# A recurrent attention layer and a mixture of experts on one core: expert weights split once and kept in f16, token tiles of 128 rows in unrolled code, and two normalisations moved to ScalarE

## The reference

```python
# block 1: linear attention with a decaying 64x64 state per head (4 heads, batch 2)
inter = einsum('bij,bcj->bci', W, rk_c) * g_p            # read of the state
S     = einsum('bcd,bkd->bck', rk_c, wk_c)               # keys are the reads, one token late
intra = einsum('bck,bkd->bcd', S * M, v_c)               # within the chunk, decayed and causal
W_new = g_C * W + einsum('bci,bcj->bij', v_c * g_w, wk_c)
x = x + out + (alpha * reads) @ W_read.T                 # out = layernorm(x)
# block 2: top 2 of 8 experts for each of 4096 tokens, width 1024
probs = softmax(layernorm(x) @ gate_w.T); p, idx = top_k(probs, 2)
h = gelu(x1n @ w1[e].T + b1[e]); y = h @ w2[e].T + b2[e] # for both chosen e
x = x + sum_k p_k * y_k
```

## Time and profile before

| | us |
|---|---|
| median of the 3 timed runs | 681.88 |
| span of the profiled execution, first to last instruction | 644.7 |
| difference: what lies around the span | 37.2 |
| PE busy | 585.2 (91%) |
| DVE busy | 560.0 (87%) |
| ACT busy | 414.1 (64%) |
| POOL busy | 291.4 (45%) |

### The profile page before, as it was taken

The page is one execution under the profiler, slowest core; times in us unless marked ns, Lnnn a source line. Parts: engine busy times, 40 slices in busy tenths (PEclk is TensorE's granted clock), DMA queues, the critical chain, the costliest instruction groups (busy, mean ns, idle before and its releaser), DMA issues.

```text
span 644.7 us, 17218 instructions
## 1 busy us (share of the span) xinstructions
PE 585.2 (91%) x5368; PEld 502.0 (78%) x5368; DVE 560.0 (87%) x1323; ACT 414.1 (64%) x819; POOL 291.4 (45%) x301
## 2 busy tenths in 40 slices
PE   3899889888894499999999999999999999999992
PEld 2677677676673288888888888888888888888882
DVE  4699898998886799999999998999999999999971
ACT  6454554543541487878777777777787877777751
POOL 4145777677667414443343434243433334342433
PEclk9899997999896599999999999999999999999997
DMA  6567464466122415253434434252524343443422
GB/s 231 185 201 280 134 229 165 161 224 205 60 94 96 97 29 84 48 76 51 73 57 67 71 53 77 47 82 47 77 49 74 51 73 57 67 72 52 80 29 33
DMA packets 87098, 63.46 MB, mean 98 GB/s; under 512 B 56224, under 2 KB 79392, under 8 KB 87072
## 3 DMA queue, kind: packets, MB, share of 16 engines
q1 hardware_dynamic: 72768, 44.23, 25.4%
q0 software_dynamic: 14304, 18.92, 17.0%
HBM read 27.36 MB, written 25.53 MB: 82 GB/s over the span
## 4 chain that ended last, share of the span: by engine, by line
PE 61%; POOL 12%; issue 11%; DVE 8%; DMA 5%; ACT 2%; POOLq 0%; DVEq 0%; ACTq 0%; SPq 0%
PE psum L1213 28%; PE psum L1194 28%; POOL sent_rows L469 6%; DMA out<-arena 3%; POOL tiny L448 2%; DMA sent_rows<-arena,tiny 2%; DVE arena L903 2%; POOL arena L477 2%; POOL out L494 1%; PE psum L1139 1%; POOL tiny L445 1%; PE psum L1113 1%; PE psum L1142 1%; DVE arena L819 1%; PE psum L1103 1%
## 5 line engine op out<-in xcount | busy, mean ns | idle before, releaser
L1194 PE MATMUL psum<-arena 128*128 128x256 f16 x1872 | 229.7, 273 | 0.7 <-ACT arena L631 0.7
L1213 PE MATMUL psum<-arena 128*128 128x256 f16 x1872 | 229.5, 273 | 0.4 <-DVE arena L996 0.4
L1009 DVE SCALAR_TENSOR_TENSOR arena<-weights,arena 128x1024 f16<-128x1024 f16 x156 | 190.2, 1221 | 25.0 <-issue 14.1
L494 POOL DMA_INDIRECT out<-arena x78 | 133.3, 1709 | 155.9 <-ACT arena L670 135.4
L1194 PEld LDWEIGHTS psum<-arena 128*128 128x128 f16 x1872 | 183.0, 98 | 23.1 <-DVE arena L1009 0.9
L1213 PEld LDWEIGHTS psum<-arena 128*128 128x128 f16 x1872 | 183.1, 98 | 21.9 <-DVE arena L996 0.7
L651 ACT ACTIVATE arena<-weights 128x1024 f16 x156 | 164.2, 1055 | 35.8 <-PE psum L1213 20.8
L631 ACT ACTIVATE arena<-psum,arena 128x256 f32<-128x256 f32 x312 | 130.7, 470 | 68.3 <-PE psum L1194 63.6
L996 DVE TENSOR_TENSOR arena<-arena 128x512 f16<-128x512 f32 x156 | 108.1, 693 | 5.3
L469 POOL DMA_INDIRECT sent_rows<-arena,tiny x64 | 63.7, 995 | 41.4 <-DVE tiny L778 21.6
L503 POOL COPY arena<-arena 128x2 int32<-128x2 int32 x39 | 24.4, 625 | 107.6 <-DMA out<-arena 98.8
(11 more groups left out here) (129 smaller groups left out, 566.6 us busy)
## 6 DMA issues: line engine op xcount, KB each, us to landing
weights<-in_experts SPq DMA_DIRECT2D x16, 1024.0 KB
arena<-in_b SPq DMA_DIRECT2D x39, 128.0 KB, 2.9
out<-arena SPq DMA_DIRECT2D x17, 256.0 KB, 2.4
arena<-in_x SPq DMA_DIRECT2D x16, 256.0 KB, 2.8
sent_rows<-pad SPq DMA_DIRECT2D x8, 265.0 KB, 7.5
out<-arena POOLq DMA_INDIRECT x78, 4.1
sent_rows<-arena,tiny POOLq DMA_INDIRECT x64
arena<-sent_rows SPq DMA_TRANSPOSE x39, 3.9
```

The costliest lines, as they stand in the source:

```text
L494: pool.indirect_dma_start(out=out, out_offset=bass.IndirectOffsetOnAxis(ap=tok_cur[:, 1 - par, c:c + 1], axis=0), in_=yout[:, 1 - par, c], ...
L1009: v.scalar_tensor_tensor(out=wcur[:, 1 - par, w + PIECE:w + 2 * PIECE], in0=weights[:, bass.ds(e * EW + part * PIECE, PIECE)], scalar=WSCA ...
L1194: last = pe.matmul(ps_h[:, s, mm], w1_of(par, k, lo, m), tileT[:, par, part], start=(n == 0), stop=(n == 3 * KD - 1))
L1213: last = pe.matmul(ps_y[:, par, c], lhs, w2_of(par, m, lo), start=(m == 0 and n == 0), stop=(m == MF - 1 and n == 2))
```

## The change

- `TILE` is 128: `NT` becomes 71, and a tile is one group of 128 rows.
- `weights` holds f16. Stage one splits each piece once, two pieces a step: ACT `split_high(2*(n-1))` and `split_high(2*(n-1)+1)`, DVE `split_low` of the same, in place, one piece's place behind the f32 source. `wcur` and its splits in stage two are gone.
- Stage two is not a loop: 71 tiles are written out. PE reads the tile's expert from the table (`value_load`) and addresses each 128 columns of w1 and each 256 columns of w2 by a register.
- `first` has four blocks of 128 hidden units a bank and moves 128 tokens; `second` has 128 tokens stationary. Bias b2 of all experts is loaded once; the gate is folded into `finish` on DVE. Tiles are loaded four ahead; POOL adds one group of rows a tile, each after the one before it has landed.
- Both normalisations go to ACT as Identity with scale and bias; POOL computes the bias (`shift`) with two small operations more for each.
- The state is 64 columns wide (`ps_state` 128x2x2x64), `faded` is gone, and DVE updates the state with `decayC` itself; reads within the chunk are issued as one group of 64-column matmuls ahead of the group that reads the state.

```diff
-TILE = 256
+TILE = 128
-EW = 4 * PIECE
+EW = 4 * 2 * PIECE
...
+            def split_high(j, m, mp):
+                loaded(a, w_in[mp], m, mp)
+                reached(a, "wlo_done", j - 1)
...
+                a.activation(to, frm, ACT.Copy, scale=WSCALE).then_inc(S["whi_done"], 1)
...
+                if active(n, 0):
+                    reached(a, "shift1_done", n)
+                    reached(a, "xT_ps", n - 2)
+                    reached(a, "res_done", n - 2)
+                    for b in range(B):
+                        last = a.activation(xn[:, par, b], xt[:, par, b], ACT.Identity, scale=rs1[:, b:b + 1],
+                                            bias=shift1[:, b:b + 1])
...
+                if active(n, 3):
+                    m = n - 3
+                    reached(a, "shift2_done", m)
...
+                        last = a.activation(xm[:, 1 - par, b], res_of(m)[:, b], ACT.Identity, scale=rs2[:, b:b + 1],
+                                            bias=shift2[:, b:b + 1])
...
-                        pool.tensor_scalar(ve, moments[:, :, 1], EPS, None, ALU.add).then_inc(S[mid], 1)
+                        pool.tensor_scalar(ve, moments[:, :, 1], EPS, None, ALU.add)
+                        pool.tensor_scalar(shift, moments[:, :, 0], -1.0, None, ALU.mult).then_inc(S[mid], 1)
...
+                        reached(pool, end, m)
+                        pool.tensor_tensor(shift, shift, rs, ALU.mult).then_inc(S[last], 1)
...
+            def split_low(j):
+                reached(v, "whi_done", j)
...
+                v.scalar_tensor_tensor(out=lo, in0=frm, scalar=WSCALE, in1=hi, op0=ALU.mult,
+                                       op1=ALU.subtract).then_inc(S["wlo_done"], 1)
...
-                    for side in range(2):
-                        d = slice(side * HD, (side + 1) * HD)
-                        last = v.tensor_tensor(state[d, :, :, d].rearrange("p b k i -> p (b k) i"),
...
+                    for k in range(KD):
+                        last = v.scalar_tensor_tensor(out=state[:, :, k], in0=state[:, :, k], scalar=decayC[:, k:k + 1],
+                                                      in1=ps_state[:, :, k], op0=ALU.mult, op1=ALU.add)
...
+            def w1_of(e, k, lo, m):
+                return halves[:, bass.ds(e * EW + ((2 * k + lo) * PIECE + m * P), P)]
+            def w2_of(e, m, lo):
+                return halves[:, bass.ds(e * EW + ((2 * (2 + m // 4) + lo) * PIECE + m % 4 * D), D)]
...
+            def first(i, e, q):
+                if q == 0:
+                    pe.wait_ge(tileT_ld[i % 4], (i // 4 + 1) * 16)
+                came(pe, "act_done", i - 1, 2, q)
+                for mm in range(4):
+                    n = 0
+                    for k in range(KD):
+                        for lo, part in ((0, k), (0, KD + k), (1, k)):
+                            last = pe.matmul(ps_h[:, q, mm], w1_of(e, k, lo, 4 * q + mm), tileT[:, i % 4, part],
+                                             start=(n == 0), stop=(n == 3 * KD - 1))
...
+            def second(i, e, q):
+                s = 2 * (i % 2) + q
+                came(pe, "split_done", i, 2, q)
+                if q == 0:
+                    came(pe, "yout_done", i - 2)
+                for mm in range(4):
+                    for n, (half, lo) in enumerate(((h_hi, 0), (h_hi, 1), (h_lo, 0))):
+                        last = pe.matmul(ps_y[:, i % 2], half[:, s, mm], w2_of(e, 4 * q + mm, lo),
...
+            for i in range(NT + 1):
+                if has(i):
+                    e_of[i] = pe.value_load(tile_exp_i[0:1, i:i + 1], min_val=0, max_val=E - 1)
+                    first(i, e_of[i], 0)
+                if has(i - 1):
+                    second(i - 1, e_of[i - 1], 0)
+                if has(i):
+                    first(i, e_of[i], 1)
+                if has(i - 1):
+                    second(i - 1, e_of[i - 1], 1)
```

466 lines of the change are left out of this document (172 added, 294 removed).

## The result

The changed kernel takes 780.69 us (778.19 to 783.33, 4 runs) and before 682.09 (680.44 to 683.91, 4 runs): a ratio of 1.143, with a 95% interval of 1.138 to 1.148. The forecast was 703, in a range of 664 to 738. The side was right, and so was the reason (PE's sequencer). The size was not.

A forecast was written before the change was run, and what follows sets the result against it. The prediction took PE to bound stage two and DVE stage one, with PE's sequencer setting the new stage two's pace. Span 644.7 +25 -3 +1.5 -2 = 666, with 37.2 around it 703 us, range 664 to 738.

The forecast's parts named there:

- stage two: Stage-two term: 71 tiles of 6.13 us, set by PE's sequencer, 435 us against 410.4, so +25 us.
- stage one and between: Stage one -3 us (bounds -8 and +12), steps going from 11.6 to about 10.95 us; larger table and first tile's wait +1.5.
- end: End of the kernel: one add in place of two and no gate on ACT, -2 us.
- sum of the span: Whole profiled span: 644.7 us with +25 -3 +1.5 -2 gives 666 us.
- Stage two, PE's sequencer: Stage two: 48 register operations, table read and waits take 6.13 us a tile against the array's 5.30; chance 0.56.
- 109 whatever follows: PE's sequencer, stage two: a register operation costs 109 ns start to start; array instructions behind it add about 2 ns each.
- The bound from above, 120 ns: Stage two: highest price of one register operation, 57 + 63 = 120 ns, which would give 462 us.
- PE's queue evens `first` against `second`: Stage two: the queue offsets `first` (3.6 us operations, 2.7 array) against `second` (1.8, 2.6) but can't hide the sum.
- Stage two, PE's array: Stage two: 128-column matmuls at 56 ns, so the array needs 5.30 us a tile, 377 us in all, 33 less.
- the array decides: Stage-two rival: register operations hidden or under 95 ns, 377 us there, 645 in all; chance 0.24, wholly or nearly (645 to 678).
- stage one gets longer by port contention: Stage-one rival: DVE splits and POOL operations share one port, no step gain, +15 to +20 us, 722 in all; chance 0.12.
- With the 37.2 us around it: Base of the sum: 37.2 us outside the profiled span, added to 666 to give 703.4 us.

The follow-up runs named there:

- e9: The kernel before, unchanged, run a third time, on the slower kind of chip: 677.2 us, 0.999 of before.
- e10: The changed kernel again, unchanged, in a set where before takes 680.04 us: 780.5 us, 1.150 of before.
- e2: The changed kernel with addresses of coming groups worked out ahead in pairs, two to a fused operation of six parts: 646.0 us, one execution.
- e1: The changed kernel with expert 0's weights for every tile, so no table read or register operation on PE: 648.7 us, one execution.
- e13: The changed kernel with each address worked out one matmul group before the group that uses it: 751.2 us, 1.104 of before.
- e3: The kernel before with only the two normalisations moved to ScalarE, with POOL's shift operations: 691.1 us, one execution.
- e4: The changed kernel with its 32 weight splits moved out of stage one to between the stages: 840.8 us, one execution.

## Why the prediction was wrong

Against e9 and e10, which share a chip, and step by step:

| term | forecast | measured | from |
|---|---|---|---|
| stage two | +25 | +101.5 | 410.4 to 511.9 |
| stage one and between | -3 +1.5 | +3.6 | 252.0 to 255.6 |
| end | -2 | -2.1 | 11.9 to 9.8 behind the last matmul |
| sum of the span | +21.5 | +103 | 674.3 to 777.2 |

The two traces are single executions, and those of before spread over 8 us in that set. By the medians (780.50 and 680.04) the difference is 100.5, so that stage one and between come to about +1: the term lies between +1 and +4.

**Stage two, PE's sequencer: the right step, mis-sized.** The failed step is the price of a register operation, "109 whatever follows", plus 0.003 for the array instructions, in a tile of 6.13 us. Measured are 0.124 and 7.21 us (mean of 40 tiles of the trace). Of the 1.08 us between:

- 48 x 0.012 = 0.58 are this price. The reading of the earlier trace rows was right for its row: that operation, with a semaphore instruction behind it, starts 109 ns before it (250.765 and 250.874). Wrong was "whatever follows", at 2 ns for each array instruction. In the changed kernel it is 124 behind one matmul and behind two, in e2 132 where nothing stands between and 152 with three or six matmuls: array instructions behind an operation cost 15 to 20 ns once. Spread over the 24 of the earlier trace rows, such a sum looks like 2 ns each. The bound from above, 120 ns, was too low too. Each ns was known to be worth 3.4 us, so 12 ns are 41 us.
- 0.13 to 0.15 are the table read: 0.53 and a wait of 0.11 were forecast; from TENSOR_LOAD at 500.986 to the next operation at 501.777 it is 0.79.
- 0.38 weren't in the sum at all: the pauses on every eighth operation. They add 10 to 160 ns to the 124, stand in `first` (71% of their time, with 67% of the operations) and in `second` alike, and recur every 8 operations, 12 loads and 12 matmuls, so every 32 instructions of PE; the longest, about 155, returns after some 62 operations. They are tied to the count of instructions, not to a full queue or a wait. Whether it is the fetching of the unrolled code, no run tells; in e1 and e2 the array sets the pace and hides them.

"PE's queue evens `first` against `second`" held: in `second`, where the array (2.6 us) is slower than the sequencer, the operations still start 124 ns apart, and the tile is the sum of the sequencer's own distances.

**Stage two, PE's array: right.** 56 ns for 128 columns and 377 us in all were forecast; e1 and e2 show 56 and 377.7 to 378.6. The 56 was a choice between bounds of 26 and 98, so that it hit to the ns is in part luck. The 81 ns of the Trainium skill (TensorE: Matmul & The Clock Gate, Back-to-back issue gap) would have made a tile of e2 6.5 us; it takes 5.3, so the measurement decides against it here. The rival "the array decides" failed for the changed kernel and describes e2: its turning point, an operation at 95 ns, was sound. Of what the Trainium skill (Advanced Engine Details and Errata, Sequencer Loop) states, that other engine instructions can be read and queued while a control instruction executes, e13 shows no gain for this stream: the operations took 124 ns each, with loads that needed nothing from them behind.

**Stage one: about right in size, for a wrong reason.** I forecast VectorE's load falling and POOL deciding, a step of 10.95 us. Before has 11.6 in its trace and the changed kernel 13.8, but on a chip like that of the timed runs e9 shows before at 14.3 (eight steps, 74 to 189 us). By blocks of scores, e10 against e9: the first is 4.5 us later (21.2 and 16.7) and the fifth 7.1 (66.3 and 59.2), for which +3 was forecast; the eleven steps behind it are 5.0 shorter (148.3 and 153.3), for which -6 was forecast from the other kind of chip; the way to the first matmul of stage two is 1.5 longer, as forecast. So the small sum is two misses that offset each other, and the steps were compared in kernels whose clock and late signals differ. The changed kernel's step is a ring. POOL ends `shift` for xn at 143.6, ScalarE's xn follows, then its exp, for which VectorE's choice of slots waits, and then the scatters:

```profile
142.52 1.09 POOL L420 TENSOR_TENSOR tiny<-tiny 128x2 f32<-128x2 f32 x1
...
147.78 1.10 POOL L441 DMA_INDIRECT sent_rows<-arena,tiny  x1 [0.97 <-POOL arena L435]
```
```profile
140.51 0.60 ACT L550 ACTIVATE arena<-psum 128x512 f32<-128x512 f32 x1 [3.95 <-PE psum L1027]
...
143.64 1.09 ACT L559 ACTIVATE arena<-arena,tiny 128x256 f32<-128x256 f32 x2 [1.59 <-POOL tiny L420]
144.64 0.20 ACT L566 ACTIVATE tiny<-tiny 128x16 f32<-128x16 f32 x1
```
```profile
142.33 1.23 DVE L651 SCALAR_TENSOR_TENSOR weights<-weights  x1 [0.23 <-ACT weights L501]
...
144.87 0.17 DVE L701 TENSOR_REDUCE tiny<-tiny 128x2 f32<-128x16 f32 x1 [1.23 <-ACT tiny L566]
```

The rival "stage one gets longer by port contention" saw a piece of this, on the other side: the splits stay at 1.22 to 1.23 us, and POOL's small operations beside them pay. L420 takes 1.09 us beside the split at 142.33 and 0.19 in its other 31 runs; L416 takes 1.13 to 1.31 in 8 of the 11 that meet a split and 0.22 alone; of 128 such operations of the four lines 14 are hit, by some 13 us in all. How much of this lies on the chain isn't shown.

**The sum: a wrong base.** "With the 37.2 us around it" took a difference of two chips for a fixed cost. What lies around the span is 1.8 us in each run of the changed kernel. The other 35 were a longer stage one of the timed executions, on another kind of chip; e9's trace, of one of the quicker executions there, has 30 of them. It did little harm by luck: the error stood in the base of both kernels. Had the changed kernel been compared with the trace alone, its stage one would seem 37 us worse, and a search for that loss would have gone astray, as my theory for e3 and e4 did in part.

## What to carry to other kernels

Count the register operations that a dynamic address puts between short matmuls, and price each by its distance from start to start among its like, not by its duration: here 124 ns for 46, so more than two matmuls of 128 columns. Take the distance with the same kind of instruction behind it as in the new code. Fuse several addresses in one operation, ahead of the group that uses them: half the operations turned a kernel 15% slower than before into one 5% faster, on the kind of chip where both were run. Before a span and a time are subtracted, see that they are of one execution; and compare two kernels on one kind of chip. Where engines pass work round a ring, an engine's list says little of what relief will bring. Before an engine's wait is called idleness, see whether what it waits for was itself waiting for that engine.

## What the runs showed of the hardware that was not expected

- A fused register operation on PE's sequencer lasts 46 ns (three parts) or 74 (six), and the next starts 124 or 152 ns after it with matmuls between, 109 (before a semaphore instruction) or 132 (before another operation) without. The rest isn't a wait for the register (e13).
- In the unrolled code of the changed kernel the sequencer pauses every 32 instructions for 10 to 160 ns more, 0.38 us a tile of 7.21.
- Loads and matmuls that read their address from a register go at 56 ns for 128 columns, as with constant addresses (e2 beside e1).
- One program has two levels by chip, 646 and 680 us. In the slower, the signal of the 64-row scores comes up to 3.9 us after its modelled end in most of the later chunks, in the quicker never (14 and 5 traces), and the granted clock is 0.80 in 140 us of stage one against 0.96.
- Twelve useless matmuls a chunk made the kernel before 0.9% faster on such a chip.
